# Second loop of a graph kernel: at most four gathers in flight in place of one pause at the eighth

## What is computed

```python
h = jnp.maximum(_layernorm(x, axis=-1), 0.0)
x_tangent = logmap0(h)
h = x_tangent @ W.T + b
deg = segment_sum(ones, dst) + segment_sum(ones, src)
dinv = jnp.maximum(deg, 1.0) ** (-0.5)
msg = h[src] * (dinv[src] * dinv[dst])[:, None]
out = segment_sum(msg, dst, num_segments=num_nodes)
x = x + expmap0(out)
```

## Time and profile before

| | |
|---|---|
| median of 3 runs | 1232.49 us (1229.73 to 1232.68) |
| the profiled execution | 1227.9 us |
| its span | 1225.7 us |
| busy: PE, PEld, DVE, ACT, POOL | 940.2, 830.7, 739.7, 392.8, 663.9 us |
| mean granted TensorE clock | 0.71 |
| 208 gathers of the second loop (L700) | 198.0 us, 952 ns each |

### The profile page before, as it was taken

The page is one execution under the profiler, slowest core; times in us unless marked ns, Lnnn a source line. Parts: engine busy times, 40 slices in busy tenths (PEclk is TensorE's granted clock), DMA queues, the critical chain, the costliest instruction groups (busy, mean ns, idle before and its releaser), DMA issues.

```text
span 1225.7 us, 22268 instructions
## 1 busy us (share of the span) xinstructions
PE 940.2 (77%) x5820; PEld 830.7 (68%) x5820; DVE 739.7 (60%) x2771; ACT 392.8 (32%) x1107; POOL 663.9 (54%) x629
## 2 busy tenths in 40 slices
PE   4466787989787888888888973568877777787776
PEld 2256686878686778777777862357766776777676
DVE  8656767666666666666666667734554544455554
ACT  1602324242423232322323221613433334344331
POOL 0266767767676767676767620254444444444441
PEclk9756666676767676767676666768877778777777
DMA  5543343434343434444443411211111111111111
GB/s 149 178 131 113 108 142 106 138 104 140 106 139 105 136 109 128 119 121 124 116 132 110 140 34 57 74 42 40 42 43 43 40 43 43 41 39 43 41 40 30
DMA packets 87848, 111.23 MB, mean 91 GB/s; under 512 B 20787, under 2 KB 65791, under 8 KB 87807
## 3 DMA queue, kind: packets, MB, share of 16 engines
q0 software_dynamic: 26624, 68.20, 20.6%
q1 hardware_dynamic: 61191, 42.64, 11.5%
HBM read 99.83 MB, written 10.95 MB: 90 GB/s over the span
## 4 chain that ended last, share of the span: by engine, by line
PE 60%; DVE 17%; issue 14%; DMA 2%; POOL 2%; another core or an unknown queue 2%; DVEq 1%; ACT 1%; SPq 0%; POOLq 0%; ACTq 0%
PE ps_q L1552 15%; PE ps_r L1564 10%; PE ps_q L1703 5%; PE ps_c L1536 4%; PE ps_q L1678 4%; PE ps_r L1694 3%; PE ps_s L1678 3%; PE ps_c L1572 2%; PE ps_f L1606 2%; POOL kv L665 2%; PE ps_b L1678 2%; PE ps_f L1605 2%; PE ps_c L1678 2%; PE ps_c L1532 2%
## 5 line engine op out<-in xcount | busy, mean ns | idle before, releaser
L665 POOL DMA_INDIRECT kv<-kv_tab,idx x416 | 465.6, 1119 | 247.9 <-issue 163.1
L700 POOL DMA_INDIRECT kv<-hs_tab,idx x208 | 198.0, 952 | 288.1 <-PE ps_q L1687 123.2
L1374 ACT ACTIVATE S<-iota,nloc 128x128 f32<-128x128 f32 x384 | 122.0, 389 | 423.1 <-PE ps_r L1564 277.9
L1552 PE MATMUL ps_q<-qwin,ST 128*128 128x128 f32 x832 | 205.8, 431 | 2.2 <-DVE ST L877 2.2
L1552 PEld LDWEIGHTS ps_q<-qwin,ST 128*128 128x128 f32 x832 | 186.5, 330 | 3.0 <-issue 2.2
L932 DVE TENSOR_TENSOR prod<-kv,ps_q 128x512 f32<-128x512 f32 (+1 forms) x128 | 74.6, 583 | 124.0 <-issue 68.1
L1564 PE MATMUL ps_r<-wv,S 128*128 128x137 f32 x832 | 139.0, 339 | 1.8 <-DVE wv L1009 1.8
L1564 PEld LDWEIGHTS ps_r<-wv,S 128*128 128x128 f32 x832 | 138.9, 251 | 2.1 <-DVE wv L1009 2.1
L1694 PE MATMUL ps_r<-qkv,xt 128*128 128x128 f32 x800 | 94.7, 280 | 0.9 <-ACT xt L1465 0.9
L1694 PEld LDWEIGHTS ps_r<-qkv,xt 128*128 128x128 f32 x800 | 93.4, 197 | 1.1 <-ACT xt L1465 1.1
L1453 ACT ACTIVATE S<-iota,nloc 128x128 f32<-128x128 f32 x208 | 67.0, 387 | 45.1 <-PE ps_q L1687 45.1
(11 more groups left out here) (257 smaller groups left out, 1666.6 us busy)
## 6 DMA issues: line engine op xcount, KB each, us to landing
dloc_b<-dloc_tab SPq DMA_DIRECT2D x32, 416.0 KB
kv<-kv_tab,idx POOLq DMA_INDIRECT x416
attr_s<-in_attr SPq DMA_DIRECT2D x32, 192.0 KB
kv<-hs_tab,idx POOLq DMA_INDIRECT x208
kv_tab<-qkv SPq DMA_DIRECT2D x5, 640.0 KB, 4.0
x_tab<-x SPq DMA_DIRECT2D x32, 64.5 KB
qwin<-q_tab SPq DMA_DIRECT2D x32, 64.0 KB
xwin<-in_x SPq DMA_DIRECT2D x32, 64.0 KB
```

The costliest lines, as they stand in the source:

```text
L665: pool.indirect_dma_start(out=kv[:, b, t, :], out_offset=None, in_=kv_tab, in_offset=bass.IndirectOffsetOnAxis(ap=idx[:, b, t:t + 1], axis ...
L700: pool.indirect_dma_start(out=kv[:, j, t, 0:D], out_offset=None, in_=hs_tab, in_offset=bass.IndirectOffsetOnAxis(ap=idx[:, j, t:t + 1], ax ...
L1374: A.activation(S[:, b, t, :], iota[:], ACT.Abs, bias=nloc[:, g, t:t + 1] if known(g) else nloc[:, bass.ds(g, 1), t:t + 1].rearrange("p g t ...
L1552: mm = M.matmul(ps_q[c % 2][:, (t - t0) * D:(t - t0 + 1) * D], ST[:, b, t, :], qwin[:, b, :], start=True, stop=True)
```

## The change

Each buffer gets four landing semaphores in place of one. Gather t raises number t % 4, and from the fifth gather on each one first waits until the gather four before it has landed. PE and DVE wait for all four instead of one. The pause at the eighth gather of this loop is gone (the first loop keeps its own). Diff, whole but for a renaming in a branch that isn't taken:

```diff
+FLIGHT = 4
...
-        s_g1 = [sem(f"s_g1{i}") for i in range(2)]
+        s_g1 = [[sem(f"s_g1{i}_{k}") for k in range(FLIGHT)] for i in range(2)]
...
+        def landed(n, j, k):
+
+            return 8 * len(range(k, T, FLIGHT)) * (n - j)
...
                 for t in range(T):
-                    if t == HALF:
-                        wait_apart(pool, s_g1[j], 8 * T * (n - j) + 16 * t, (s_tab[0], 32 * 3))
+                    if t >= FLIGHT:
+                        wait_apart(pool, s_g1[j][t % FLIGHT], landed(n, j, t % FLIGHT) + 16 * (t // FLIGHT), (s_tab[0], 32 * 3))
                     pool.indirect_dma_start(out=kv[:, j, t, 0:D], out_offset=None, in_=hs_tab,
                                             in_offset=bass.IndirectOffsetOnAxis(ap=idx[:, j, t:t + 1], axis=0))\
-                        .then_inc(s_g1[j], 16)
+                        .then_inc(s_g1[j][t % FLIGHT], 16)
...
                 if far:
-                    dve.wait_ge(s_g1[j], 8 * T * (n + 2 - j))
+                    for k in range(FLIGHT):
+                        dve.wait_ge(s_g1[j][k], landed(n + 2, j, k))
                     set_idx(2 * n + 5, j, s_idx1)
...
-                pe.wait_ge(s_g1[j], 8 * T * (n + 2 - j))
+                for k in range(FLIGHT):
+                    pe.wait_ge(s_g1[j][k], landed(n + 2, j, k))
```

More of the change, by code:

```diff
@@ L439, in build @@
             s_dfac, s_fac, s_facd, s_z, s_p, s_wv, s_agg, s_agg1, s_rc, s_R)
-        s_e_got1 = s_g1
+        s_e_got1 = s_g1[0][0:2]
         (s_n_got1, s_n_z1, s_n_ss1, s_n_norm1, s_n_th1, s_n_y1, s_n_put1, s_n_own1) = (
```

## The result

| | before | change |
|---|---|---|
| median, runs side by side | 1231.61 us (1229.73 to 1232.68, 4 runs) | 1267.41 us (1261.77 to 1268.03, 4 runs) |
| ratio, 95% interval | | 1.0282 (1.0249 to 1.0315): slower |
| the profiled execution, its span | 1227.9, 1225.7 us | 1268.03, 1266.0 us |
| second loop, first gather to last instruction | 438.3 us | 477.3 us |
| one batch's first gather to the next one's, mean of batches 3 to 15 | 26.9 us | 29.1 us |

The change is slower by 2.8%.

The account below looks back on a forecast made before the run. The prediction took PE to bound the second loop, its count-stage stalls on the path. Profiled 1227.9 us plus 40 us (2.9 us in 14 batches), with pause and added waits at nothing, gave 1268 us; range 1172 to 1300.

Parts of the forecast that it names:

- The forecast's case: Whole kernel: one longer PE stall per batch makes it slower, 1268 us, own range 1238 to 1300, chance 0.52.
- The limit of four by itself will hardly ever hold a gather back: Pool's second-loop gathers: the gather four back started 5.0 us before and lands within about 2.3, at most 3.2 us.
- The pause lay in Pool's slack: Pool, before the eighth gather: removing it saves 2.0 us per batch, hidden by 9.3 us of waiting for PE.
- One stall per batch in PE's count stage: Sign beside Pool's batch: one stall from about 6 to 17 us after its start, stage 19 to 20 us for 16.8.
- SP's two loads: Sign in SP's queue: loads take 0.70 us, as in a stall, where 0.34 is usual outside one.
- and then stands at its next wait: PE's count stage: all queues crawl while Pool's queue waits, handed-over gathers are unfinished and PE runs bf16 matmuls; 7.6 us per batch.
- 2.9 us per batch in 14 batches, 40 us: PE's count stage ends 24.7 us after the batch's start for 21.8; bounds nothing to 7 us per batch, 98 us.
- an example of a long stall: Prologue's second batch, before the change: no pause after the first, PE crawls 6.75 us with 8 matmuls; supports 2.9 us.
- Fewer in flight, no stalls: Rival, PE's count stage: at most four never start the crawl, 97 us less, 1131 us, or 1182 us; chance 0.30.
- they go on while one or two gathers are left: Argument against the rival "Fewer in flight, no stalls": PE's stalls continue with only one or two gathers left.
- Nothing moves: Rival, second loop: the limit doesn't bind and the stalls stay, 1227.9 to 1232 us; chance 0.18.
- The Trainium skill's rule named there: Under "Nothing moves": a taken branch outside the instruction window waits for a fetch, so stalls sit at the loop's code.

Follow-up runs that it names:

- experiment 8: The kernel before with its mid-batch pause taken out of both loops, on a chip with stalls: 1508.5 us, ratio 1.196.
- experiment 12: The change with a limit of three gathers in flight for four, on a chip with stalls: 1303.2 us, ratio 1.035.
- experiment 1: The kernel before with the second loop's pause taken out, one signal kept, on the chip without stalls: 1055.9 us, ratio 0.969.
- experiment 2: The change with its nine Pool waits per batch put on a long-met semaphore, on the chip without stalls: 1056.4 us, ratio 0.971.
- experiment 10: The change with the pause at the eighth gather kept as well, on a chip with stalls: 1267.0 us, ratio 1.003 to the kernel before.
- experiment 11: The kernel before with four memsets of a spare tile in place of the second loop's pause, on a chip with stalls: 1256.7 us, ratio 0.9975.
- experiment 9: The kernel before with two pauses per second-loop batch, before the fifth and ninth gathers, on a chip with stalls: 1204.5 us, ratio 0.953.
- experiment 7: The change with a limit of two gathers in flight for four, on a chip with stalls: 1181.3 us, ratio 0.937.
- experiment 5: The change run again unaltered, on a chip with stalls: 1300.0 us, ratio 1.034 to the kernel before.
- experiment 4: The kernel before with its pause but four signals for one, waited for by Pool, PE and DVE, on the chip without stalls: 1092.8 us, ratio 1.003.
- experiment 6: The kernel before, unaltered, on a chip with stalls: median 1265.9 us, its profiled run 1288.7 us.

## Why the prediction was right, and where it wasn't

**The number.** 1268 was predicted against the profiled execution, and 1268.03 was measured; the ratio of 1.0282 agrees with the 2.9% of the text. The forecast's case came in. But so close a hit is luck: the cause was named wrongly, and three terms were off in opposite ways.

**Pool.** "The limit of four by itself will hardly ever hold a gather back" is right: gaps of 0.30 us, and experiments 8 and 12 show that neither four nor three binds. The pause lay in Pool's slack, as said, and its 2.0 us of Pool's time were worth nothing on the chips with stalls. On the chip without them a pause was worth 3%, in the other direction (experiment 1). The prediction had no such case, since it took one chip's trace for the kernel.

**The stall.** "One stall per batch in PE's count stage, from about 6 to 17 us after the batch's first gather, and the stage at 19 to 20 us" came in as one stall from 5.7 to 18.4 us and a stage of 19.9. It ended 3.2 us after the thirteenth gather's start, where 2.3 was put, and let 8 matmuls through for 11. The free rest was put at 7.4 us for 81 matmuls and took 7.22 for 89. One of the signs given didn't: SP's two loads, said to go at 0.70 us, mostly fell outside the stall.

**The cause is the step that failed.** The text read the stalls as the time in which Pool's queue has handed gathers over "and then stands at its next wait", with gathers unfinished and PE in bf16 matmuls, and so made the nine added waits guilty. Experiment 8, without any such wait, has the same second loop; experiment 2's waits cost nothing where nothing stalls; and experiments 10 and 11 bring the kernel before back by adding the pause to the nine waits, or by a gap without a landing wait; and experiment 9's stall is in fp32 matmuls. What the runs bear out is: **on the chips with stalls, PE comes to crawl beside an unbroken run of gathers, and goes on crawling until the run has been broken and has landed; the pause was such a break in the middle of the batch.** DVE crawls too in some of these stretches, later than PE; Pool doesn't. The effect on this change is the same by either reading, one long stall for two short ones, and so the sum held. For any other edit the two part: the first reading would have sent a reader to take waits away (experiment 8: 20% slower with both pauses gone), the second to add gaps (experiment 7: 6% faster).

**The terms.** 2.9 us per batch in 14 batches, 40 us, against 2.2 us in 13, 9.3 us in the prologue and 1.3 at the end, 39 us. The stage grew by 3.2 us in the median and 3.6 in the mean (16.3 to 19.9), but a pair has other parts: outside the stage it took 10.5 us before and 9.1 after, in the mean, so over a third was given back. That goes with the higher granted clock behind the stage, a term that the prediction left out. The prologue was read as an example of a long stall and not costed; there, the lost drain joined 26 gathers in one run. These misses cancelled.

**The rivals.** "Fewer in flight, no stalls" had the right picture of the end, a full drain, and the wrong condition: fewer than four in flight isn't it, as experiment 12 shows. With a limit that does bind, two, it comes in part: the second loop is 83 us shorter, where this rival had 97 (on another chip, whose loop before was 438.3 us). The prediction set "they go on while one or two gathers are left" against it; that fits a crawl that lasts until the drain just as well. "Nothing moves" fell: the stalls moved with Pool's gaps. The Trainium skill's rule named there (Runtime: NRT & Kernel Launch, Instruction fetch mechanics) doesn't explain them, since experiment 11's two stalls and the change's one stand in the same loop code of PE.

**Open.** What starts a crawl. It began 6.2 and 4.6 us into the two runs of a batch in the kernel before, in the change no later than 5.7 us, and in experiment 9 once after 3.1 us; in the prologue of the kernel before, the first eight gathers of a run (798.14 to 807.05) went out beside 50 fp32 matmuls (L1694, from 799.48) that took 8.19 us, no more than the 8.47 us of the same 50 in the changed kernel with no gather beside them, and the stall came only then, 11.7 us into the run. So neither a number of gathers nor the type of the matmuls sets it alone. Why one chip has none is open too, and why the second loop's length is the same (442.7 to 442.8 us) on the two others.

The traces differ in one more way. That of experiment 1, on the chip without stalls, holds 19595 semaphore updates of engines and 14950 of DMAs, that of the kernel before 9768 and 6170, for the same 87862 DMA packets; experiments 5 and 11 have 8893 and 9106 engine updates. On the chips with stalls half or more of these records are missing. Every time on record comes with such a trace's span and clock, so no run tells whether the recording has a part in the stalls. It is an untested rival for their origin, though not for what the pause does to them.

## What to carry to other kernels

A pause that looks like slack on its own engine can be what lets another engine run: before it is taken out, look at what the others do in the microseconds behind it. Stalls marked "issue" on several engines at once, that end when a run of indirect gathers has landed, can be answered by gaps in the run: a limit in flight that really binds, or 2 us of other work put between gathers (here memsets). And such an edit has to be timed on more than one chip: taking out the same pause made the kernel 3% faster on one (experiment 1) and the second loop 41 us longer on another (experiment 8).

## What the runs showed of the hardware

- **Chips differ by up to 16% on one kernel.** The kernel before takes 1088.4 us on one chip (mean granted TensorE clock 0.755), and 1231.6, 1254.5 and 1265.9 us in the three other sets of runs (0.70 to 0.71 in the profiles). Most of it is in the second loop, 311.4 us in experiment 4 for 442.7 in experiment 6, with the stalls there gone and the granted clock at 0.94 for 0.76 in this loop.
- **The stall has a grain.** In it PE starts an instruction every 0.7, 1.4, 2.1 or 2.8 us (906.96 and 908.39, 913.40 and 915.48, up to 919.71 in the changed kernel), while the DMA engines are busy for only a fifth of the time (0.19 in the stretch from 906.96).
- **An indirect gather of 128 rows** starts every 1.25 us in an unbroken run, on all chips, and has landed 2.2 to 2.5 us after its start (959.82 to the last landing at 962.07 in experiment 7, 929.88 to 932.38 in the kernel before). The Trainium skill (DMA: Bandwidth & Descriptors, Anatomy of one DMA) fits 2.0 us plus bytes / 436e3 for one DMA from GpSimd, an estimate of 2.15 us for the 64 KB of one gather. The trace agrees with it or lies up to 0.35 us above.
- **The clock is not the cause of the stall, but it pays part of it back.** The granted clock in the stall is 0.68 and in the free stretch behind it 0.62, lower, while matmuls go through at 12 per us. On the chip without stalls the stage ran at the full clock. Behind the stage the granted clock was 1.00 in the changed kernel (926.93 to 935.90) and 0.86 before (907.32 to 917.82), worth 1.5 us in that pair.
